# Front of a conditioned attention stack: partition maxima by TensorE, softmax bias by ScalarE, a symmetric score table made in part, new orders

## Chip, cores, metric

One core of a Trainium2 chip. The metric is the device time of one execution in microseconds. All eight batches are worked by this one core. Below, PE is TensorE, DVE VectorE, ACT ScalarE and POOL GpSimd.

## What is computed

The reference works on `x` of 8 x 256 x 256 (batch, tokens, features), in float32. Cut to what matters:

```python
# 1. conditioning: layer norms with gathered gains, six parts, MLP, layer norm
y = mlp_ln(concat([w0*h, w1*t, w2*m, w3*n, w4*r, w5*s]))
# 2. attention with L2-like similarity, 16 heads of 16
q_row_2 = max(sum(abs(q), -1), -1) ** 2          # per batch and head
k_col_2 = max(sum(abs(k), -2), -1) ** 2
denom = sqrt(sum(q*q)) * max(sum(abs(y), -2), -1)
sim = -(q_row_2 - 2*q@k.T + k_col_2) / denom
x1 = x + softmax(sim) @ v @ W_proj + b_proj
# 3. attention of each token over its own 16 heads; q = k = v = kx
kx = modulated_linear(x1, cond)                  # 16 heads of 16
scores[n, h, j] = sum_d kx[n, h, d] * kx[n, j, d] / 4
x2 = modulated_linear(softmax(scores) @ kx, cond)
# 4. six layers of windowed attention and gated MLP
return x1 + layers(x2)
```

`scores[n, h, j]` equals `scores[n, j, h]`. In `sim` the terms that depend on neither token are the same for a whole row.

## The kernel before

Three parts run one after the other, with a barrier of all engines between: `front` (steps 1 to 3), `local_layers` (step 4) and `write_out`.

In `front` each engine has a queue of its own, written by a loop over `t` in `range(FRONT_STEPS)`. Each stage has an offset: `pairs(t, off)` runs it in every step, for one pair of heads (64 pairs: 8 per batch), `batches(t, off)` in every eighth step, for one batch, `once` one time. Within a step the stages stand in the order of the lines of the loop. The queues are in-order and meet in semaphores only, so step 40 of one engine need not run beside step 40 of another. A batch passes through conditioning (a), attention (b) and the token's heads (c), and up to five batches are under way.

Stages that matter here, with their lines:

- Per pair of heads: PE `scores` (L559) makes 128x1024 scores; DVE `softmax` takes the maximum (`rmax`, L1107) and makes `rbias` of it in three operations of 128x4 (L1112 to L1114: times the scale, plus `offset`, minus `offset`); ACT `softmax` (L822) takes four exponentials of 128x256 with their sums; PE `flip_p` (L571) turns half of them into one bank, ACT `flip_p` (L831) copies that to `pr_t`, PE `weigh` (L584) multiplies by `v`. `scores` of pair j waits for the exponentials of pair j-2.
- Per batch, sizes of q, k and y: ACT sums into `qsq`, `kab`, `yab`; PE `sizes` (L541, L543) makes 16 matmuls of four columns and a sum over partitions; DVE puts 33 columns into `most` (128x33) and the norm into `fro` (L1085); POOL `scale_root` (L315) takes `fro` to the power -0.5, POOL `peaks` (L308) is a `partition_all_reduce` (maximum) of `most`; DVE `scales` (L1090 to L1097) makes `scl` and `offset`, 128x16 each.
- Conditioning: POOL `gather` (six indirect DMAs), `scale_h`, `scale_t`, `scale_s`, `affine_h` (elementwise, 128x512), PE `flip_x`, `flip_t`, `flip_s`, `flip_h` (L399), then `mixer_hidden` (L489, 32 matmuls of 256 columns). In the same queue of POOL stand `root` (L270), `dem_root` (L252, once), `turn_k` and `head_out` (L330).
- Heads of a token, per half u and quarter k: DVE `head_prod` (L1162, a product of 128x1024) and `head_scores` (L1169, its sum over 16, giving 128x64), then per half `head_peak`, ACT `head_exp`, DVE `head_weights`; then POOL `head_out` (L330) and DVE `head_out` (L1192) in turn.

PE's results of a whole batch share two banks, M0 and M1. `BANK0` and `BANK1` list their uses in order, and `after` makes a use wait for the copy of the one before it.

The write-out turns `state` by PE into one of two banks, ACT copies it into one of two row tiles, SP stores it.

## Time and profile before

| | |
|---|---|
| median of 3 runs | 3747.55 us (3742.12 to 3752.66) |
| profiled execution | 3748.91 us, span of its trace 3747.6 us |
| busy PE / DVE / ACT / POOL | 3447.7 / 2700.4 / 2549.3 / 2039.9 us |
| last `state` of the front begins | 827.7 us |
| first transpose of the write-out | 3734.2 us |
| granted clock of PE, mean | 0.934 |

The page cuts the span into 40 slices of 93.7 us; the digits of a slice are tenths of busy time, those of PEclk tenths of the full clock. PEld is PE's weight load, which overlaps PE. "Idle before" is what an engine stood still for ahead of an instruction, with the work that ended it; "issue" there means that nothing in the profile released it.

### The profile page before, as it was taken

Reading aid. Unit: us, or ns where it says so; the run is one execution under the profiler, and the core shown is the slowest. Engines: PE = TensorE matmul, PEld = TensorE weight load, DVE = VectorE, ACT = ScalarE, POOL = GpSimd, SP = SyncE. Lnnn points to the kernel's source line nnn. Section 1 sums busy time; section 2 is a strip of 40 time slices with the busy share of each in tenths; the row PEclk is TensorE's granted clock in tenths of the full one; section 3 lists DMA queues with packets and bytes.
Section 4 is the critical chain, followed back from the end, with each engine's and each line's share of the span. In section 5 each row is a group of like instructions: output and inputs, shape, how many; then the busy total and the mean of one; then the engine's idle time right before and its main releaser. Section 6 shows DMA issues by size and latency. Waiting matters only on the chain. (4 is left out here: it accounts for less than half of the span.)

```text
span 3747.6 us, 85444 instructions
## 1 busy us (share of the span) xinstructions
PE 3447.7 (92%) x32080; PEld 3019.9 (81%) x32080; DVE 2700.4 (72%) x5351; ACT 2549.3 (68%) x7091; POOL 2039.9 (54%) x1544
## 2 busy tenths in 40 slices
PE   5898889928999999999999999999999999999997
PEld 4787777716888888888888888888888888888886
DVE  2358777776777787777877778767787777877773
ACT  1554455406877777777777777777777777787774
POOL 5325453345655566555565555655556555565652
PEclk8687778658999999999999999999999999999998
DMA  3110000001000010000100001000010000100000
GB/s 112 50 32 29 29 29 4 4 20 49 18 2 2 10 45 19 2 2 10 40 24 2 2 10 37 27 2 2 10 37 27 2 2 10 37 26 7 4 7 23
DMA packets 26935, 75.60 MB, mean 20 GB/s; under 512 B 4025, under 2 KB 9753, under 8 KB 25497
## 3 DMA queue, kind: packets, MB, share of 16 engines
q1 hardware_dynamic: 21360, 52.89, 4.3%
q0 software_dynamic: 4864, 16.78, 1.4%
q8 instruction: 260, 4.26, 0.5%
q14 instruction: 147, 1.20, 0.1%
q10 hardware_dynamic: 304, 0.47, 0.0%
HBM read 65.94 MB, written 4.19 MB: 19 GB/s over the span
## 5 line engine op out<-in xcount | busy, mean ns | idle before, releaser
L1495 POOL TENSOR_TENSOR rnorm<-norm,half 128x8 f32<-128x8 f32 x384 | 684.4, 1782 | 1149.8 <-DVE norm L1927 1149.8
L1750 ACT ACTIVATE prob<-ps_s,ebias,rnorm 128x128 f32<-128x128 f32 x1536 | 681.3, 458 | 39.3 <-DVE ebias L1939 38.1
L1932 DVE TENSOR_REDUCE negmax<-ps_s 128x4 f32<-128x512 f32 x384 | 264.2, 688 | 404.8 <-PE ps_s L1574 404.4
L1497 POOL TENSOR_TENSOR turned<-by_cos,turned 128x512 f32<-128x512 f32 x384 | 515.3, 1342 | 0.0
L1740 ACT ACTIVATE qk_t<-ps_t 128x512 f32<-128x512 f32 x384 | 230.9, 601 | 271.4 <-PE ps_t L1545 271.4
L1520 PE MATMUL ps_qk<-w_hi,x_hi 128*128 128x512 f32 x768 | 333.1, 434 | 70.9 <-DVE turned L1919 56.8
L1614 PE MATMUL ps_f<-attn_t,w_o 128*128 128x128 f32 x3072 | 358.7, 275 | 0.0
L1614 PEld LDWEIGHTS ps_f<-attn_t,w_o 128*128 128x128 f32 x3072 | 350.5, 192 | 0.1
L1946 DVE TENSOR_TENSOR prob<-prob,rinv 128x512 f32<-128x512 f32 x384 | 322.2, 839 | 13.2
L1658 PE MATMUL ps_f<-lin_hi,w_hi 128*128 128x256 f32 (+1 forms) x1056 | 312.0, 295 | 6.4 <-DVE state L2008 6.4
L1750 ACT ACTIVATION_READ_ACCUMULATOR prob<-ps_s,ebias,rnorm 128x1 f32 x1536 | 315.3, 205 | 0.0
L1520 PE MATMUL ps_qk<-w_lo,x_hi 128*128 128x512 f32 x768 | 305.8, 398 | 0.0
L1723 ACT ACTIVATE sq<-ps_qk 128x512 f32<-128x512 f32 x384 | 230.0, 599 | 110.6 <-PE ps_qk L1520 107.3
L1520 PE MATMUL ps_qk<-w_hi,x_lo 128*128 128x512 f32 x768 | 304.3, 396 | 0.0
L1658 PE MATMUL ps_f<-lin_lo,w_hi 128*128 128x256 f32 (+1 forms) x1056 | 297.7, 282 | 0.0
L1500 POOL TENSOR_TENSOR turned<-turned,rnorm 128x256 f32<-128x256 f32 x384 | 280.3, 730 | 30.1
L1658 PE MATMUL ps_f<-lin_hi,w_lo 128*128 128x256 f32 (+1 forms) x1056 | 296.3, 281 | 0.0
L1919 DVE TENSOR_TENSOR turned<-ps_qk,sin_t 128x256 f32<-128x256 f32 x768 | 285.9, 414 | 0.0
L1759 ACT ACTIVATE prob_t<-ps_t 128x512 f32<-128x512 f32 x384 | 229.3, 597 | 60.1 <-PE ps_t L1583 60.1
L1913 DVE TENSOR_TENSOR by_cos<-ps_qk,cos_t 128x512 f32<-128x512 f32 x384 | 263.7, 687 | 3.7 <-ACT sq L1723 3.2
L1924 DVE TENSOR_REDUCE norm<-sq 128x8 f32<-128x512 f32 x384 | 259.5, 676 | 0.0
L1583 PE MATMUL ps_t<-ident,prob 128*128 128x128 f32 x1536 | 251.7, 286 | 4.4 <-DVE prob L1946 4.4
(263 smaller groups left out, 9685.4 us busy)
## 6 DMA issues: line engine op xcount, KB each, us to landing
w_raw<-in_w_qkv SPq DMA_DIRECT2D x24, 768.0 KB, 4.7
w_raw<-in_w SPq DMA_DIRECT2D x12, 693.0 KB, 4.5
w_o<-in_w_o SPq DMA_DIRECT2D x6, 1024.0 KB, 4.8
w_raw<-in_w SPq DMA_DIRECT2D x6, 768.0 KB, 4.2
x_tok<-in_x SPq DMA_DIRECT2D x8, 256.0 KB
kept<-x_t SPq DMA_DIRECT2D x8, 256.0 KB
w_raw<-kept SPq DMA_DIRECT2D x8, 256.0 KB, 2.7
out<-rows_out SPq DMA_DIRECT2D x8, 256.0 KB, 2.2
```

Of the source, the lines that this page charges most:

```text
L1495: G.tensor_tensor(rnorm[:, i % 4, :], norm2[:, k, :], half[:, :], ALU.pow).then_inc(s["rnorm"], 1)
L1497: G.tensor_tensor(turned[:, k, :], by_cos[:, k, :], turned[:, k, :], ALU.add).then_inc(s["turned"], 1)
L1500: G.tensor_tensor(kk, kk, rnorm[:, i % 4, GH:].unsqueeze(2).broadcast_to([P, GH, DH]), ALU.mult).then_inc(s["k_unit"], 1)
L1520: last = E.matmul(out, lhs.bitcast(F32R), w[:, kt, g, columns].bitcast(F32R), start=n == 0, stop=n == len(terms) - 1)
L1614: last = E.matmul(ps_f[0][:, mt * N + u * P:][:, 0:P], w_o[:, j, T(mt)], attn_t[:, j, T(u)], start=j == 0, stop=j == INNER // P - 1)
L1658: last = E.matmul(f[0:cut.stop - cut.start, part * N:(part + 1) * N], w[:, kt, cut].bitcast(F32R), x[:, kt, :].bitcast(F32R), start=n == 0 ...
L1750: last = A.activation(prob[:, k, h, :], half_bank(h % 2)[:, T(h // 2)], ACT.Exp, bias=ebias[:, k, h:h + 1], scale=rnorm[:, i % 4, h:h + 1] ...
L1913: V.tensor_tensor(by_cos[:, k, :].rearrange("p (a h d) -> p a h d", a=2, h=GH), qk[:, :].rearrange("p (a h d) -> p a h d", a=2, h=GH), cos ...
L1919: last = V.tensor_tensor(heads(turned[:, k, cut]), heads(qk[:, cut])[:, :, ::-1, :], sn.broadcast_to([P, GH, 2, DH // 2]), ALU.mult)
L1924: V.tensor_reduce(norm2[:, k, :], sq[:, k, :].rearrange("p (h d) -> p h d", d=DH), AX.X, ALU.add).then_inc(s["norm2"], 1)
L1932: V.tensor_reduce(negmax[:, k, :].rearrange("p (c o) -> p o c", o=2), ps_s[:, :, 0:2 * P].rearrange("p o (c k) -> p o c k", c=2), AX.X, AL ...
L1946: V.tensor_tensor(prob[:, k, :, :], prob[:, k, :, :], rinv[:, k, :].unsqueeze(2).broadcast_to([P, GH, P]), ALU.mult).then_inc(s["prob_unit ...
```

## The change

- Maxima over partitions: `peaks` goes. DVE still fills `most`; PE `flip_most` turns its columns into rows of 16 partitions (`M1`), with the sum of `qmask` behind them; DVE `take_peaks` takes the maxima there; POOL `scale_root` works on 16x1; DVE `scales` makes two columns of 16 partitions, and PE `scale_row` spreads them over 128 partitions; DVE `take_scales` copies them.
- Bias: DVE `softmax` keeps the maximum only. ACT makes `rbias` in two activations of 128x2 per pair, ahead of its exponentials, and waits for them on a semaphore.
- Heads: quarter k makes only the columns from 4k on (1024, 768, 512, 256 products). ACT `head_mirror` copies the other three blocks of each half (16, 32, 48 columns), and `head_peak` waits for it.
- Orders: all offsets and the order of the lines in the loops of POOL, PE, ACT, DVE are new, and so is the order of uses of M0 and M1; 142 steps.
- Write-out: eight banks and eight row tiles, and one semaphore.

```diff
...
-    m["most"], m["peak"] = sb("most", [P, 2 * NH + 1]), sb("peak", [P, 2 * NH + 1])
-    m["peak2"], m["yrec"] = sb("peak2", [P, 2 * NH]), sb("yrec", [P, 1])
-    m["offset"], m["qmask"] = sb("offset", [P, 2, NH]), sb("qmask", [P, NH])
-    m["fro"], m["scl0"], m["scl"] = sb("fro", [P, NH]), sb("scl0", [P, NH]), sb("scl", [P, 2, NH])
+    m["most"], m["peak"] = sb("most", [P, 2 * NH + 1]), sb("peak", [NH, 3])
+    m["peak2"], m["yrec"], m["scol"] = sb("peak2", [NH, 2]), sb("yrec", [NH, 1]), sb("scol", [NH, 2])
+    m["qmask"] = sb("qmask", [P, NH])
+    m["fro"], m["scl0"], m["scl"] = sb("fro", [NH, 1]), sb("scl0", [NH, 1]), sb("scl", [P, 2, 2 * NH])
...
-    m["prod"], m["prodo"] = sb("prod", [P, 2, 4, NH, HD]), sb("prodo", [P, 2, 4, HD, NH])
+    m["prod"], m["prodo"] = sb("prod", [P, 2, 4 * NH * HD]), sb("prodo", [P, 2, 4, HD, NH])
...
-FRONT_STEPS = 123
+FRONT_STEPS = 142
...
+    BANK0 = (("scale_row", 7, "scl", 1), ("mixer_hidden", 6, "hid", 1), ("flip_o", 8, "o_t", 1), ("dem_row", 8, "w_k", 1),
+             ("flip_y", 6, "y_t", 1), ("flip_heads", 10, "o2_t", 1), ("q1", 6, "q", 2), ("k1", 6, "k", 2), ("sizes", 6,
+             "most", 1), ("flip_x", 5, "x_t", 1), ("flip_s", 5, "cat_s", 1))
+    BANK1 = (("flip_h", 6, "cat_h", 1), ("mixer_out", 6, "y_b", 1), ("project_out", 8, "x1", 1), ("token_k", 8, "kx", 1),
+             ("q0", 6, "q", 2), ("heads_out", 10, "ostate", 1), ("k0", 6, "k", 2), ("project_v", 6, "v", 1), ("flip_t", 5,
+             "cat_t", 1), ("flip_most", 6, "peak", 1))
...
-        def peaks(a):
-            G.wait_ge(s["kmask"], a + 1)
-            G.wait_ge(s["fro"], a + 1)
+        def scale_root(a):
+            G.wait_ge(s["peak"], a + 1)
             if a:
-                G.wait_ge(s["scl"], a)
-            G.partition_all_reduce(m["peak"][:, :], m["most"][:, :], P, bass.bass_isa.ReduceOp.max
-                                   ).then_inc(s["peak"], 1)
-
-        def scale_root(a):
-            G.wait_ge(s["fro"], a + 1)
-            if a:
-                G.wait_ge(s["scl"], a)
-            G.tensor_tensor(m["scl0"][:, :], m["fro"][:, :], m["nhalf"][:, 0:NH], ALU.pow).then_inc(s["scl0"], 1)
+                G.wait_ge(s["scl_col"], a)
+            G.tensor_tensor(m["scl0"][:, :], m["fro"][:, :], m["nhalf"][0:NH, 0:1], ALU.pow).then_inc(s["scl0"], 1)
...
-            E.wait_ge(s["qmask"], a + 1)
             E.wait_ge(s["q_abs"], a + 1)
             after(BANK0, "sizes", a)
             for u in range(NU):
                 for t in range(NTILE):
-                    E.matmul(M0[:, NH * (1 + u) + 4 * t:][:, 0:4], m["q_abs"][:, t, T(u)], m["slots"][:, :],
-                             start=True, stop=True)
-            E.matmul(M0[:, 0:NH], m["ones"][:, :], m["qmask"][:, :], start=True, stop=True).then_inc(s["size_ps"], 1)
+                    last = E.matmul(M0[:, NH * u + 4 * t:][:, 0:4], m["q_abs"][:, t, T(u)], m["slots"][:, :],
+                                    start=True, stop=True)
+            last.then_inc(s["size_ps"], 1)
+
+        def flip_most(a):
+
+            most = m["most"]
+            E.wait_ge(s["qmask"], a + 1)
+            E.wait_ge(s["kmask"], a + 1)
+            E.wait_ge(s["most"], a + 1)
+            after(BANK1, "flip_most", a)
+            E.transpose(M1[0:NH, T(0)], most[:, 0:NH], ident[:, :])
+            E.transpose(M1[0:NH, T(1)], most[:, NH:2 * NH], ident[:, :])
+            E.matmul(M1[0:NH, T(2)], most[:, 2 * NH:].broadcast_to([P, NH]), ident[:, :], start=True, stop=True)
+            E.matmul(M1[0:NH, 3 * P:3 * P + 1], m["qmask"][:, :], m["ones"][:, 0:1], start=True, stop=True
+                     ).then_inc(s["most_ps"], 1)
+
+        def scale_row(a):
+            E.wait_ge(s["scl_col"], a + 1)
+            after(BANK0, "scale_row", a)
+            for k in range(2):
+                last = E.matmul(M0[:, k * NH:(k + 1) * NH], m["scol"][:, k:k + 1].broadcast_to([NH, P]), ident[0:NH, 0:NH],
+                                start=True, stop=True)
+            last.then_inc(s["scl_ps"], 1)
...
-            A.wait_ge(s["rbias"], j + 1)
+            A.wait_ge(s["rmax"], j + 1)
+            if hp == 0:
+                A.wait_ge(s["scl"], b + 1)
             if j >= 2:
+                A.wait_ge(s["exp"], j - 1)
                 A.wait_ge(s["prt_ps"], 2 * j - 2)
             if hp == 0 and b >= 2:
                 A.wait_ge(s["pri"], b - 1)
+            for e in range(2):
+                h = slice(2 * hp + e, 2 * hp + e + 1)
+                z = slice(NH + 2 * hp + e, NH + 2 * hp + e + 1)
+                last = A.activation(rbias[:, j % 2, e, :], rmax[:, j % 2, e, :], ACT.Identity, scale=scl[:, b % 2, h],
+                                    bias=scl[:, b % 2, z])
+            steps[0] += 1
+            last.then_inc(s["act_step"], 1)
+            A.wait_ge(s["act_step"], steps[0])
...
+        def head_mirror(c, u):
+            of = sc[:, 2 * (c % 2) + u, :, :]
+            A.wait_ge(s["hs"], 8 * c + 4 * u + 4)
+            for k in range(1, 4):
+                last = A.activation(of[:, 4 * k:4 * k + 4, 0:4 * k], of[:, 0:4 * k, 4 * k:4 * k + 4].rearrange("p j h -> p h j"),
+                                    ACT.Copy)
+            last.then_inc(s["hm"], 1)
...
         def take_sizes(a):
             V.wait_ge(s["size_ps"], a + 1)
             if a:
-                V.wait_ge(s["peak"], a)
+                V.wait_ge(s["most_ps"], a)
+            V.tensor_reduce(most[:, 0:NH], M0[:, 0:2 * NH].rearrange("p (u h) -> p h u", u=NU), AX.X, ALU.max
+                            ).then_inc(s["most"], 1)
+
+        def take_peaks(a):
+            V.wait_ge(s["most_ps"], a + 1)
+            if a:
                 V.wait_ge(s["scl0"], a)
-            V.tensor_reduce(most[:, 0:NH], M0[:, NH:3 * NH].rearrange("p (u h) -> p h u", u=NU), AX.X, ALU.max)
-            V.tensor_copy(m["fro"][:, :], M0[:, 0:NH]).then_inc(s["fro"], 1)
+                V.wait_ge(s["scl_col"], a)
+            V.tensor_reduce(m["peak"][:, :], M1[0:NH, 0:3 * P].rearrange("p (a n) -> p a n", a=3), AX.X, ALU.max)
+            V.tensor_copy(m["fro"][:, :], M1[0:NH, 3 * P:3 * P + 1]).then_inc(s["peak"], 1)
 
         def scales(a):
-            peak, peak2, sl, of = m["peak"], m["peak2"], scl[:, a % 2, :], offset[:, a % 2, :]
+
+            peak, peak2, col = m["peak"], m["peak2"], m["scol"]
             V.wait_ge(s["peak"], a + 1)
-            V.reciprocal(m["yrec"][:, :], peak[:, 2 * NH:])
-            done(V.tensor_tensor(peak2[:, :], peak[:, 0:2 * NH], peak[:, 0:2 * NH], ALU.mult))
+            if a:
+                V.wait_ge(s["scl_ps"], a)
+            V.reciprocal(m["yrec"][:, :], peak[:, 2:3])
+            done(V.tensor_tensor(peak2[:, :], peak[:, 0:2], peak[:, 0:2], ALU.mult))
+            done(V.tensor_tensor(col[:, 1:2], peak2[:, 0:1], peak2[:, 1:2], ALU.add))
+            V.wait_ge(s["scl0"], a + 1)
+            done(V.tensor_scalar(col[:, 0:1], m["scl0"][:, :], m["yrec"][:, 0:1], 2.0, ALU.mult, ALU.mult))
+            done(V.scalar_tensor_tensor(out=col[:, 1:2], in0=col[:, 1:2], scalar=0.5, in1=col[:, 0:1], op0=ALU.mult,
+                                        op1=ALU.mult))
+            V.tensor_tensor(col[:, 1:2], col[:, 1:2], col[:, 1:2], ALU.subtract).then_inc(s["scl_col"], 1)
+
+        def take_scales(a):
+            V.wait_ge(s["scl_ps"], a + 1)
             if a >= 2:
                 V.wait_ge(s["exp"], HP * (a - 1))
-            done(V.tensor_tensor(of, peak2[:, 0:NH], peak2[:, NH:], ALU.add))
-            V.wait_ge(s["scl0"], a + 1)
-            done(V.tensor_scalar(sl, m["scl0"][:, :], m["yrec"][:, 0:1], 2.0, ALU.mult, ALU.mult))
-            V.scalar_tensor_tensor(out=of, in0=of, scalar=0.5, in1=sl, op0=ALU.mult, op1=ALU.mult).then_inc(s["scl"], 1)
+            V.tensor_copy(scl[:, a % 2, :], M0[:, 0:2 * NH]).then_inc(s["scl"], 1)
 
         def softmax(j):
-            b, hp = divmod(j, HP)
-            k, of_heads = j % 2, [P, 2, NU]
-            sl = scl[:, b % 2, 2 * hp:2 * hp + 2].unsqueeze(2).broadcast_to(of_heads)
-            of = offset[:, b % 2, 2 * hp:2 * hp + 2].unsqueeze(2).broadcast_to(of_heads)
             V.wait_ge(s["sc_ps"], j + 1)
             if j >= 2:
                 V.wait_ge(s["exp"], j - 1)
-            V.tensor_reduce(rmax[:, k, :, :], SB[:, 2 * k:2 * k + 2, :].rearrange("p e (u n) -> p e u n", u=NU), AX.X, ALU.max,
-                            negate=True).then_inc(s["rmax"], 1)
-            V.wait_ge(s["rmax"], j + 1)
-            if hp == 0:
-                V.wait_ge(s["scl"], b + 1)
-            done(V.tensor_tensor(rbias[:, k, :, :], rmax[:, k, :, :], sl, ALU.mult))
-            done(V.tensor_tensor(rbias[:, k, :, :], rbias[:, k, :, :], of, ALU.add))
-            V.tensor_tensor(rbias[:, k, :, :], rbias[:, k, :, :], of, ALU.subtract).then_inc(s["rbias"], 1)
+            V.tensor_reduce(rmax[:, j % 2, :, :], SB[:, 2 * (j % 2):2 * (j % 2) + 2, :].rearrange("p e (u n) -> p e u n", u=NU),
+                            AX.X, ALU.max, negate=True).then_inc(s["rmax"], 1)
...
+        def among(k):
+
+            return prod[:, k % 2, :][:, 0:4 * (NH - 4 * k) * HD].rearrange("p (h j d) -> p h j d", h=4, d=HD)
+
         def head_prod(c, u, k):
             if u == 0 and k == 0:
                 V.wait_ge(s["kx"], c + 1)
             if c + u + k // 2:
                 V.wait_ge(s["hs"], 8 * c + 4 * u + k - 1)
-            kh, hs = kx[:, u, :].rearrange("p (h d) -> p h d", d=HD), slice(4 * k, 4 * k + 4)
-            V.tensor_tensor(prod[:, k % 2, :, :, :], kh[:, hs, :].unsqueeze(2).broadcast_to([P, 4, NH, HD]),
-                            kh.unsqueeze(1).broadcast_to([P, 4, NH, HD]), ALU.mult).then_inc(s["hp"], 1)
+            kh, shape = kx[:, u, :].rearrange("p (h d) -> p h d", d=HD), [P, 4, NH - 4 * k, HD]
+            V.tensor_tensor(among(k), kh[:, 4 * k:4 * k + 4, :].unsqueeze(2).broadcast_to(shape),
+                            kh[:, 4 * k:, :].unsqueeze(1).broadcast_to(shape), ALU.mult).then_inc(s["hp"], 1)
 
         def head_scores(c, u, k):
             V.wait_ge(s["hp"], 8 * c + 4 * u + k + 1)
             if c >= 2:
                 V.wait_ge(s["ho_prod"], 8 * (c - 2) + 4 * u + 4)
-            V.tensor_reduce(sc[:, 2 * (c % 2) + u, 4 * k:4 * k + 4, :], prod[:, k % 2, :, :, :], AX.X, ALU.add).then_inc(s["hs"], 1)
+            V.tensor_reduce(sc[:, 2 * (c % 2) + u, 4 * k:4 * k + 4, 4 * k:], among(k), AX.X, ALU.add).then_inc(s["hs"], 1)
 
         def head_peak(c, u):
-            V.wait_ge(s["hs"], 8 * c + 4 * u + 4)
+            V.wait_ge(s["hm"], 2 * c + u + 1)
...
-    rows_out = ctx.enter_context(nc.sbuf_tensor("rows_out", [P, 2, NU, D], F32))
-    bank = [ctx.enter_context(nc.psum_tensor(f"out_bank{k}", [P, 512], F32)) for k in range(2)]
-    s = Signals(nc, ctx, "end", "flipped rows stored0 stored1")
+    rows_out = ctx.enter_context(nc.sbuf_tensor("rows_out", [P, B, NU, D], F32))
+    bank = [ctx.enter_context(nc.psum_tensor(f"out_bank{k}", [P, 512], F32)) for k in range(B)]
+    s = Signals(nc, ctx, "end", "flipped rows stored")
...
```

New order of POOL in the steps of one period (steps 80 to 87; in brackets the batch, for head_out then half and quarter): 80 head_out(0; 1,0), head_out(0; 1,1), scale_t(4), affine_h(4); 81 gather(5); 82 head_out(0; 1,2); 84 scale_root(3), head_out(0; 1,3); 85 turn_k(1); 86 head_out(1; 0,0), (0,1), root(4,y), root(5,x), scale_h(5), head_out(1; 0,2), scale_s(5); 87 head_out(1; 0,3), root(5,h).

PE around the boundary: 86 project_v(4); 87 weigh, sizes(4), flip_t(5), flip_p, flip_x(5), weigh, scores, flip_most(4), flip_p, flip_s(5); 88 weigh, flip_h(5), flip_p, weigh, scores, scale_row(4), flip_p, mixer_hidden(5). DVE: 85 head_out(1; 0,3); 86 h_norm(5), take_sizes(4); 87 head_out(1; 1,0), yk_most(4), softmax, take_peaks(4), scales(4); 88 take_scales(4). At the start POOL has dem_root ahead of root(0,x) in step 46, and scale_root(0) in step 60, behind affine_h(1) in 56 and gather(2) in 57.

## Rows read from the trace of the kernel before

**Rows 1.** The page, 40 slices of 93.7 us: busy tenths and granted clock.

```profile
PE   5898889928999999999999999999999999999997
PEclk8687778658999999999999999999999999999998
```

**Rows 2.** Windows: length, busy us of PE, PEld, DVE, ACT, POOL, clock, DMA.

```profile
98.70:166.60 67.90, 58.30 (x324) 49.17 (x323) 23.46 (x65) 38.51 (x115) 21.80 (x20) 0.75 0.10 32
166.60:241.00 74.40, 73.78 (x418) 64.63 (x417) 37.02 (x79) 43.45 (x123) 24.69 (x21) 0.78 0.11 37
...
324.80:415.10 90.30, 76.24 (x399) 65.92 (x398) 64.37 (x106) 44.05 (x126) 44.56 (x29) 0.74 0.08 27
...
673.20:731.00 57.80, 50.84 (x260) 42.98 (x260) 47.30 (x71) 27.05 (x77) 21.06 (x10) 0.65 0.01 5
731.00:829.00 98.00, 33.60 (x116) 26.57 (x116) 82.21 (x80) 12.95 (x29) 52.11 (x22) 0.56 0.01 3
```

**Rows 3.** Timeline of POOL at one batch boundary: start us, us, instruction, idle before.

```profile
405.25 3.83 POOL L315 TENSOR_TENSOR scl<-fro,nhalf 128x16 f32<-128x16 f32 x1 [9.86 <-DVE fro L1085]
415.13 0.47 POOL L308 PARTITION_ALL_REDUCE peak<-most  x1 [6.05 <-issue]
422.62 2.31 POOL L330 TENSOR_TENSOR prodo<-sc,kd 128x1024 f32<-128x1024 f32 x1 [7.02 <-issue]
424.90 1.25 POOL L284 TENSOR_TENSOR hh<-hh,ct 128x512 f32<-128x512 f32 x1
```

**Rows 4.** Timeline of PE at the same boundary.

```profile
417.24 0.66 PE L571 MATMUL bank_pb<-ident,pr 128*128 128x128 f32 x4
427.56 1.12 PE L399 MATMUL bank_m<-ident,hh 128*128 128x128 f32 x4 [9.66 <-POOL hh L285]
```

**Rows 5.** Waits of the front (0 to 860 us): us in total, times, longest.

```profile
ACT pr_t L831 <- PE bank_pb L571: 151.9, 72, 10.0
...
PE bank_m L399 <- POOL hh L285: 55.8, 7, 11.3
...
POOL peak L308 <- issue: 47.1, 8, 6.0
```

**Rows 6.** Windows of 10 us around the same boundary.

```profile
400.00:410.00 10.00, 10.00 (x49) 9.46 (x48) 5.36 (x11) 6.98 (x28) 3.83 (x1) 0.56 0.01 2
...
430.00:440.00 10.00, 10.00 (x48) 9.14 (x48) 9.93 (x9) 5.48 (x14) 4.42 (x2) 0.50 0.00 1
```

**Rows 7.** Timeline of POOL at the start of the front.

```profile
74.63 5.42 POOL L252 TENSOR_TENSOR dem<-dem_v,nhalf 128x32 f32<-128x32 f32 x1
```

**Rows 8.** Groups by line and form, 0 to 860 us: count | busy, mean ns | idle.

```profile
L1162 DVE TENSOR_TENSOR prod<-kx 128x1024 f32<-128x1024 f32 x64 | 88.4, 1387 | 0.0
...
L1169 DVE TENSOR_REDUCE sc<-prod 128x64 f32<-128x1024 f32 x64 | 77.4, 1210 | 0.0
...
L1113 DVE TENSOR_TENSOR rbias<-rbias,offset 128x4 f32<-128x4 f32 x64 | 27.1, 423 | 2.2
...
L768 ACT ACTIVATE y_t<-bank_m,fcols 128x256 f32<-128x256 f32 x16 | 8.2, 560 | 14.8 <-PE bank_m L399 14.8
...
L714 ACT ACTIVATE m_hid<-bank_ob,fcols 128x8 f32<-128x8 f32 x6 | 1.1, 274 | 18.2 <-PE bank_ob L406 18.2
```

**Rows 9.** Timeline of DVE, one bias operation by itself.

```profile
457.62 0.16 DVE L1113 TENSOR_TENSOR rbias<-rbias,offset 128x4 f32<-128x4 f32 x1
```

**Rows 10.** Groups of DVE by form in the drain, 731 to 829 us.

```profile
L1162 DVE TENSOR_TENSOR prod<-kx 128x1024 f32<-128x1024 f32 x13 | 22.7, 1756 | 0.0
L1169 DVE TENSOR_REDUCE sc<-prod 128x64 f32<-128x1024 f32 x14 | 16.9, 1206 | 0.0
```

**Rows 11.** Timeline of the write-out.

```profile
3734.20 3.74 PE L2091 MATMUL out_bank<-ident,state 128*128 128x128 f32 x16 [1.96 <-PEq L2076]
...
3738.23 0.60 ACT L2100 ACTIVATE rows_out<-out_bank 128x512 f32<-128x512 f32 x1 [1.45 <-DMA out<-rows_out]
...
3738.88 1.97 PE L2091 MATMUL out_bank<-ident,state 128*128 128x128 f32 x8 [0.94 <-ACT rows_out L2100]
```

551 lines of the change are left out of this document (275 added, 276 removed).

## Prediction

> **What bounds the kernel now.** I read the page first, by its 40 slices [rows 1]. From about 910 us on (slice 10) TensorE (PE) is at 9 tenths and its granted clock at 9 or more: that is the six layers, and no edit touches them. The first nine slices, up to 829 us, are the front, where PE's digit is 8 or 9 but the clock moves between 5 and 8. So the front is where time can come from; the write-out behind the layers is the only other place.
>
> Second view: the front cut at the eight starts of the partition all-reduce, one per batch [rows 2]. The seven periods sum to 574.5 us (98.7 to 673.2), then 57.8 us until the last maximum of the scores and 98 us of drain. In a full period (324.8 to 415.1) PE is busy 76.2 of 90.3 us at a clock of 0.74, VectorE (DVE) 64.4, ScalarE (ACT) 44.0, GpSimd (POOL) 44.6. None is full: it is a pipeline of in-order queues that stops somewhere. In the drain DVE is busy 82.2 of 98 us and PE 33.6: there DVE is the bound.
>
> Third view, where it stops: POOL's timeline [rows 3] and PE's [rows 4] at one batch boundary. POOL waits 9.9 us for `fro`, takes 3.8 us for a power over 128x16, stands 6.05 us before the all-reduce with nothing released (issue), 0.47 us in it, and then 7.02 us more before its next instruction: 17.4 us from 405.25 to 422.62 for one batch's peaks. `affine_h` of the next batch is queued behind that; PE's `flip_h` waits for it 9.66 us. The waits of the whole front [rows 5] say that it is so in every batch: 47.1 us of issue before the eight all-reduces, 55.8 us of PE behind `hh`.
>
> Fourth view: what the stall costs beyond itself. Four `flip_p` transposes take 0.66 us before it and the four of `flip_h` 1.12 us after it [rows 4]: the granted clock has gone from 2.4 to 1.2 GHz. It is still 0.50 from 430 to 440 us, with PE busy throughout [rows 6]. An earlier fall belongs to `sizes` (from 401 us, 16 matmuls of four columns): mean 0.56 from 400 to 410 us. In a period of length T with mean clock c, T(1-c) is the time lost to the low level: 90.3 x 0.26 = 23.5 us from 324.8 on, 74.4 x 0.22 = 16.4 us from 166.6 on [rows 2]. Taking this and PE's idle time (14.1 and 0.6 us) away leaves 53 and 57 us of PE work at the full clock; part of the idle time lies in the low level and is taken off twice, so I take 58.
>
> **The change part by part.**
>
> *Peaks.* Removed from POOL: the all-reduce with its 6 us before and 7 us behind, and the power over 16 columns (3.8 us [rows 3]). In its place: one power over 16x1. A power over 128x32 takes 5.4 us and over 128x16 3.8 [rows 3, 7], so 0.1 us per column and about 2.2 fixed by these two, which is the upper end; zero is the lower. The all-reduce's own 0.47 shows that POOL has cheaper instructions. I take 0.7, below the middle, since the path now feeds 16 lanes in place of 128. PE gets three turns, one column of sums, two row spreads, and loses the two `ones` matmuls of `sizes`: four more at about 0.3 us (the four 128-column transposes of `flip_h` take 1.12 us at the low clock [rows 4]), with waits +1.5 us per batch. DVE gets `take_peaks`, one more small operation in `scales`, and `take_scales`: five at about 0.16 us [rows 9], under 1 us. The chain from `sizes` to `scl` is then: take_sizes, flip_most, take_peaks, root, four small DVE steps, scale_row, take_scales, about 4 us if every engine is free, against 10.4 us on POOL alone now (405.25 to 415.60).
>
> Are they free? POOL's new order puts before `scale_root` of batch a: head_out(1,0), head_out(1,1), scale_t and affine_h of a+1, gather of a+2 (six issues and a copy, some 8.5 us), head_out(1,2). A `head_out` product takes 2.31 us, an elementwise operation of 512 columns 1.25 [rows 3]. Counted from DVE's step 85, where the last release of these falls, that is 4.6 + 2.5 + 2.5 + 8.5 + 2.3 = 20.4 us, against two steps and a half (of 9 us each, an eighth of a period: 22 us) until `take_peaks`. So `scales` waits between 0 and 6 us; DVE and, one step later, ACT's softmax wait with it, and PE's `scale_row` stands in front of flip_p and the mixer. I take 3 us of PE idle per batch in place of some 13.
>
> *Bias by ACT.* DVE loses three 128x4 operations per pair. One takes 0.16 us when alone [rows 9], but the middle one 0.42 us on average, 27.1 us in all [rows 8]: between 0.5 and 1.3 us per pair, and I take 1.0, with the gaps 8.3 us per batch. ACT gets two activations of 128x2 with both scale and bias from memory. The rows [rows 8] give 0.27 us for 128x8 with a bias, and 0.56 us for 128x256 with both, so 0.27 to 0.56 and, since two columns are nearer to eight than to 256, 0.33; two with the wait on themselves 0.7 us, 5.6 us per batch, 45 us in all. ACT goes from 44 to 50 us per period, then 52 with the mirror: covered as long as the period is above 60. The Trainium skill speaks against this edit: "ScalarE: Activation LUTs", section "Rules for kernel authors", gives adds and multiplies to VectorE, since ScalarE's fixed cost per instruction is the higher. By the rows it is, 0.3 against 0.16 us; the fixed figures of that page of the Trainium skill would give about 0.37 us each, an estimate from its 186 ns and 93 ns for each of the two operands, with which ACT would still be covered and the sum the same. That rule is rival 3 here: what matters is who waits in ACT's queue.
>
> *40 of 64 columns.* The 64 products (1.387 us) and 64 sums (1.210 us) of 1024 elements [rows 8] become 1024, 768, 512 and 256. With 0.15 us fixed (by the 0.16 us of a tiny operation [rows 9]) the mean of an undisturbed 1.21 us falls to 0.81: 128 x 0.40 = 51 us less DVE in all, 6.4 per batch. ACT gets three copies per half (16 to 48 columns, 0.3 us each), 1 us, and `head_peak` waits for them, once per half, about 1.3 us in the chain of a batch's heads. Steady state: DVE 64 - 8.3 - 6.4 = 50 us per period, so it was no bound and is none; the gain of both DVE edits is worth nothing there except for shorter waits in between. Their cover gone, in the drain, they count in full.
>
> *New orders.* `project_v` comes before `sizes`; all between `sizes` and the mixer stays thin (flips of 128 and weights of 16 columns). So I keep one fall of the clock per batch there: of the 16 to 24 us lost per period, 11 stay. At the start `dem_root` (5.4 us at 74.6 us [rows 7]) is now ahead of root x of batch 0, where it was behind everything, and the first `scale_root` is behind the second gather: together the first softmax comes 5 us later.
>
> *Write-out.* Eight banks and eight row tiles in place of two. Now: 13.4 us from the first transpose to the end, since from the third batch on each pair waits for a store, ACT 1.45 us each time [rows 11]. After: 32 transposes at the measured 1.97 us per 8 are 7.9 us, then 0.6 of ACT and 2.2 of the last store (the page's time to landing of the stores to `out`): 10.7. Bounds: 9 us if stores and ACT hide all but PE, 13.4 if eight stores together are slower than one. I take -3.
>
> **The sum.** Start +5. Periods: PE work 58, new matmuls 1.5, idle 3, clock 11 make 74 for the five full periods; 66 and 70 for the two first (67.9 and 74.4 now, no heads yet). 506 in place of 574.5: -68. Last batch -8 (its low clock is 0.65, and DVE, busy 47.3 of 57.8 us, is relieved of 14 us). Drain: 13 products and 14 sums lie in it [rows 10]: 27 x 0.375 x 1.07 = 11 us, half of the 0.55 us by which the products (1.756 us) are held up there (3.5), the last bias 1.7, and 2 for shorter chains: -18. Write-out -3. Together -92. The profiled execution took 3748.91 us (span 3747.6, 1.4 above the median of the runs): 3748.9 - 92 = 3657.
>
> **The rivals.**
>
> 1. *A wait takes the stall's place.* If POOL comes to `scale_root` some 10 us late each batch, PE idles at `scale_row`, and the clock falls twice per batch as now: period about 83 for the full ones, -10 to -15 in the seven. With the other terms: -39, 3710 us. For it: the order above, and POOL's 9.9 us of waiting in front of its root now [rows 3]. Against: with 41 us of work POOL has some 30 us of idle time per period once the all-reduce is gone.
> 2. *The clock holds.* With no stall PE stays at 2.4 GHz through `sizes` too: period 63, -133 in the seven, -157 in all, 3592 us. For it: most of the low level now lies behind the stall. Against: in the second period PE is busy 73.8 of 74.4 us, without a stall, and the clock is still 0.78 [rows 2].
> 3. *ACT becomes the queue that stops, and the kernel slower.* The mirror waits for the sums (DVE) in ACT's in-order queue; behind it are `flip_p` copies, and PE's one bank of turned probabilities waits for these. ACT's copies already wait 151.9 us for PE [rows 5], so they have slack. The second mirror of a batch stands in ACT's step 72, its last sums in DVE's step 73 behind `y_add`, which waits for PE. There are 16 mirrors: from 92/16 = 5.8 us of blocked PE at each on, all is lost; at 10 us each the time is 3657 + 160 = 3817 us. Against: PE takes up the next probabilities a step later, and the first mirror has its sums a step ahead.
> 4. *Nothing moves:* the order, not POOL, holds the period. Then only the write-out and half of the drain (POOL's eight products of 2.3 us bound its end) count against the start: +5 - 9 - 3 = -7, 3742 us.
>
> **How the numbers follow.** Forecast (3630 to 3685) 0.55, rival 1 0.22, rival 2 0.14, rival 3 0.04, rival 4 0.05. The unknown costs (root 0 to 2.2 per batch, ACT 0.54 to 1.12 per pair, write-out -4 to 0) move the sum by some 10 us; period and clock by 4 us per period, 28. The range runs from 3600 (most of rival 2 below it is left out) to 3708 (half of rival 1 inside). A measurement of this kernel tells about 0.3%, 11 us: faster 0.92, within 0.04 (most of rival 4), slower 0.04.
>
> **What would show it.** Right: POOL free of the 17 us hold; `flip_h` on PE waiting under 2 us; starts of `scale_row` 72 to 77 us apart in full periods; DVE near 50 us per period; front's end (last `state` of the front) near 740 us; the last 13.4 us now under 11. Wrong: waits of PE on `scol` or of DVE on `scl0` over 5 us per batch (rival 1), mean clock over 0.9 in the periods (rival 2), ACT waiting for DVE's `sc` above 5 us with PE idle on `pr_t` (rival 3).

## The result, and the profile after

| | before | after |
|---|---|---|
| median | 3746.31 us (3742.12 to 3752.66) | 3602.68 us (3601.89 to 3603.45) |
| ratio of the two | | 0.9615, 95% interval 0.9599 to 0.9632 |
| span of the profiled execution | 3747.6 us | 3602.1 us |
| granted clock of PE, mean | 0.934 | 0.959 |

The change takes 144 us, 3.85%. Forecast were 92 us and 3657 us; the range (3600 to 3708) holds the time by 2.7 us. By the spans, 143 of the 145.5 us lie in the front and the write-out. The page of the kernel after, its slices of 90 us (to compare with [rows 1]): the clock now reaches 9 tenths in two slices of the front.

```profile
PE   4999999389999999999999999999999999999997
PEclk8789987699999999999999999999999999999998
```

Windows of the kernel after, cut at the eight `scale_root` and then at the last maximum of the scores and the last `state`, with the columns of [rows 2]:

```profile
103.10:167.48 64.38, 59.94 (x326) 51.57 (x327) 18.11 (x42) 44.77 (x131) 18.89 (x19) 0.77 0.15 49
167.48:235.61 68.13, 67.49 (x406) 58.54 (x405) 31.10 (x62) 46.74 (x136) 19.82 (x20) 0.83 0.14 40
235.61:303.62 68.01, 67.77 (x424) 59.69 (x423) 48.35 (x85) 49.19 (x147) 38.12 (x28) 0.85 0.11 38
303.62:368.85 65.23, 63.87 (x436) 56.05 (x434) 50.58 (x85) 51.11 (x153) 40.46 (x30) 0.94 0.13 42
368.85:432.94 64.09, 62.35 (x412) 55.18 (x414) 52.95 (x84) 49.82 (x148) 40.42 (x29) 0.92 0.12 42
...
561.76:608.78 47.02, 44.21 (x261) 38.48 (x260) 34.71 (x53) 31.66 (x97) 19.76 (x9) 0.72 0.02 6
608.78:688.22 79.44, 35.51 (x126) 28.58 (x126) 57.28 (x70) 14.92 (x42) 47.27 (x20) 0.56 0.01 4
```

A full period is 63 to 65 us in place of 90, and PE is busy in nearly all of it: PE is now the bound. The seven periods end at 561.76, so they take 458.7 us in place of 574.5. The terms of the span, before against after: start +4.4 (98.70, the first all-reduce, to 103.10, the first root; the first exponential goes from 101.9 to 107.7 us), periods -115.8, last batch -10.8, drain -17.3 (731.00 to 827.7 against 608.78 to 688.22), layers -2.3, write-out -3.8: together the 145.5 us between the spans, to the rounding.

POOL's timeline at one batch boundary, for [rows 3]: `affine_h` of the next batch, (six DMA issues,) a product of a head, the root over 16x1, the next product. The 17.4 us hold is gone.

```profile
356.77 1.26 POOL L284 TENSOR_TENSOR hh<-hh,ct 128x512 f32<-128x512 f32 x1
...
366.57 2.33 POOL L321 TENSOR_TENSOR prodo<-sc,kd 128x1024 f32<-128x1024 f32 x1
368.85 0.57 POOL L306 TENSOR_TENSOR scl<-fro,nhalf 16x1 f32<-16x1 f32 x1
```

Waits of the front (0 to 720 us), for [rows 5]. PE's wait for `hh` is not in the list any more, ACT's for PE has gone from 151.9 to 32.0 us, and the two that my rivals 1 and 3 named are small: DVE for POOL's root 2 us per batch, the mirror (`sc` L867) for DVE twice.

```profile
ACT pr_t L855 <- PE bank_pb L580: 32.0, 33, 2.2
...
DVE scol L1140 <- POOL scl L306: 14.3, 7, 5.1
...
ACT sc L867 <- DVE sc L1215: 11.4, 2, 9.3
...
PE bank_m L550 <- DVE scol L1143: 6.6, 3, 3.2
```

Groups of the front by form, for [rows 8]: ACT's bias and DVE's longest product.

```profile
L838 ACT ACTIVATE rbias<-rmax,scl 128x2 f32<-128x2 f32 x128 | 42.4, 384 | 30.9 <-DVE scl L1149 21.2 <-issue 9.7
L1208 DVE TENSOR_TENSOR prod<-kx 128x1024 f32<-128x1024 f32 x16 | 23.9, 1492 | 0.3
```

The write-out, for [rows 11]: 32 transposes without a stop, 9.65 us from here to the span's end at 3602.1 in place of 13.4.

```profile
3592.45 6.12 PE L2139 MATMUL out_bank<-ident,state 128*128 128x128 f32 x32 [1.96 <-PEq L2126]
```

### The profile page after: what moved, and what is told of

The parts are those of the page before. It is cut to its first block and busy times, and to the rows that moved or that the text cites. A ratio compares the mean times of both kernels' runs of the same rounds, so it can differ in the third digit from the quotient of the medians.

```text
span 3602.1 us, 85564 instructions
## 1 busy us (share of the span) xinstructions
PE 3383.3 (94%) x32144; PEld 2970.1 (82%) x32144; DVE 2583.0 (72%) x5183; ACT 2595.5 (72%) x7267; POOL 2014.8 (56%) x1536
## 5 line engine op out<-in xcount | busy, mean ns | idle before, releaser
L321 POOL TENSOR_TENSOR prodo<-sc,kd 128x1024 f32<-128x1024 f32 x64 | 162.4, 2548 | 180.3 <-DVE o L1238 98.5
```

## The experiments

All times are medians; each ratio is to the kernel before, run on the same chip. Us saved is (1 - ratio) x 3748. Differences between the runs are given by this column unless the text says that they are of medians.

| | orders | maxima | DVE's work | us | ratio, interval | saved |
|---|---|---|---|---|---|---|
| before | old | all-reduce | old | 3746 | | |
| before_copied_peaks | old | none, a copy | old | 3676.3 | 0.9799 (0.9773, 0.9825) | 75 |
| before_turned_peaks | old | turned | old | 3750.3 | 1.0009 (0.9997, 1.0021) | -3 |
| before_light_dve | old | all-reduce | light | 3713.2 | 0.9902 (0.9871, 0.9934) | 37 |
| old_work_new_orders | new | all-reduce | old | 3670.0 | 0.9791 (0.9768, 0.9813) | 78 |
| after_dve_work_back | new | turned | old | 3654.9 | 0.9745 (0.9716, 0.9773) | 96 |
| after_old_peaks | new | all-reduce | light | 3613.7 | 0.9638 (0.9622, 0.9654) | 136 |
| after_all_columns | new | turned | bias by ACT | 3628.8 | 0.9668 (0.9633, 0.9703) | 124 |
| after_bias_by_dve | new | turned | 40 columns | 3629.6 | 0.9669 (0.9636, 0.9703) | 124 |
| after | new | turned | light | 3602.7 | 0.9615 (0.9599, 0.9632) | 144 |
| after_filler | new | turned | light | 3584.1 | 0.9553 (0.9534, 0.9572) | 168 |
| after_root_first | new, 2 moves | turned | light | 3577.8 | 0.9540 (0.9520, 0.9559) | 172 |
| after_row_sizes | new | turned, other `sizes` | light | 3577.7 | 0.9535 (0.9518, 0.9552) | 174 |
| rows_and_root_first | new, 2 moves | turned, other `sizes` | light | 3574.0 | 0.9534 (0.9517, 0.9551) | 175 |

The new write-out (3.8 us by the trace, not run by itself) goes with the new orders.

### Which part is it?

**Maxima alone, in the old orders.** First the all-reduce taken out (what it computes is left out), then the turned maxima put in, at places that I chose in the old orders.

```diff
-            G.partition_all_reduce(m["peak"][:, :], m["most"][:, :], P, bass.bass_isa.ReduceOp.max
-                                   ).then_inc(s["peak"], 1)
+            G.tensor_copy(m["peak"][:, :], m["most"][:, :]).then_inc(s["peak"], 1)
```

> The kernel before with one instruction changed: POOL copies most into peak (128x33) in place of the all-reduce over partitions, so each partition keeps its own maximum (this part of the computation is left out). The power over 128x16 and all orders stay. Theory A (POOL's stand around the all-reduce, and the low clock behind it, is most of the gain): about 13 us of the 17.4 us hold go in each of eight batches, of which 8 to 13 us reach the period; 3746 becomes 3645 to 3680 us. Theory B (the new orders are most of the gain): 3725 us or more. Theory C (less work for DVE is most of it): 3725 us or more as well.

> The kernel before with the turned maxima alone: flip_most, take_peaks, scale_root on 16x1, scale_row and take_scales put into the old orders; bias by DVE, 64 columns and the old write-out stay. Theory A: 3640 to 3670 us, the period 72 to 77 us. Theory B: 3720 us or more. Theory C: 3720 us or more. If it stays above the run with the copied maxima by over 15 us, the longer way through PE and DVE costs what POOL gives back.

Theory A held for the first and fell with the second. Windows between two roots, the kernel with the copy first, the one with turned maxima second; below them PE's wait in the second, from 230 to 560 us (us, times, longest), then what DVE and POOL did ahead of one of these waits:

```profile
367.77:446.30 78.53, 71.22 (x410) 61.85 (x409) 69.07 (x107) 44.47 (x127) 45.60 (x30) 0.83 0.12 34
```
```profile
411.21:499.84 88.63, 78.81 (x418) 67.64 (x416) 71.84 (x110) 44.59 (x126) 41.03 (x28) 0.73 0.10 31
```
```profile
PE bank_m L551 <- DVE scol L1121: 22.4, 4, 7.0
```
```profile
411.43 3.85 DVE L1116 TENSOR_TENSOR scol<-peak 16x1 f32<-16x1 f32 x1
...
415.56 1.06 DVE L1119 SCALAR_TENSOR_TENSOR scol<-scol 16x1 f32<-16x1 f32 x1
416.65 2.25 DVE L1121 TENSOR_TENSOR scol<-scol 16x1 f32<-16x1 f32 x1
```
```profile
411.21 0.55 POOL L307 TENSOR_TENSOR scl<-fro,nhalf 16x1 f32<-16x1 f32 x1 [13.01 <-DVE fro L1106]
411.73 2.32 POOL L322 TENSOR_TENSOR prodo<-sc,kd 128x1024 f32<-128x1024 f32 x1
414.02 1.25 POOL L284 TENSOR_TENSOR hh<-hh,ct 128x512 f32<-128x512 f32 x1
415.35 1.26 POOL L285 TENSOR_TENSOR hh<-hh,ct 128x512 f32<-128x512 f32 x1
416.57 2.32 POOL L322 TENSOR_TENSOR prodo<-sc,kd 128x1024 f32<-128x1024 f32 x1
```

Without the all-reduce the period goes from 90.3 to 78.5 us: the hold did bound the kernel before. With the turned maxima in its place it is 88.6: PE's wait for `hh` is replaced by one for `scol`, up to 7.0 us, with the clock at 0.73.

This looks like my rival 1, but it is not: POOL was not late. It had stood for 13.01 us when `fro` came, and took the root at once. What was slow is DVE's chain behind it. Three operations over 16x1 took 3.85, 1.06 and 2.25 us; the same three take 0.15 us each in the kernel after (median of the eight batches). Each of the three ends within 0.02 us of an operation of POOL: at 415.28, 416.62 and 418.90 us, where POOL's `hh`, `hh` and product end at 415.27, 416.61 and 418.89. The excess is 6.7 us, and PE's wait there is 6.57. It is the same in the periods that begin at 322.8 and 499.8 us. So the place that I chose put DVE's chain beside POOL's products and `hh`, which the new orders do not: there POOL's next product after the root begins only at 373.79 us, when the chain is done. That another place in the old orders would have let the turned maxima pay was not tried.

**The new orders with all the old work**, and **the changed kernel with the old maxima.** (In the second the offset stays in the bias; it is the same for a whole row.) The code of the old work stands at the places of the new:

```diff
             for q in batches(t, 60):
                 scale_root(q)
+                peaks(q)
...
-            for q in batches(t, 55):
-                flip_most(q)
-            for q in batches(t, 56):
-                scale_row(q)
```

> The changed kernel with all of the old work put back in the new orders: all-reduce and power over 128x16 by POOL in the place of the new scale_root, bias by DVE, 64 columns, no mirror; only orders and write-out are new. Theory A: 3700 to 3750 us, since POOL still holds 17 us per batch. Theory B: 3610 to 3650 us. Theory C: 3690 to 3730 us.

> The changed kernel with the old maxima alone put back (sizes with its sum by ones, power over 128x16 and all-reduce by POOL, scales on 128x16); bias by ACT, 40 columns and the new orders stay. Theory A: 75 to 110 us come back, 3678 to 3713 us, and the clock in the periods falls to about 0.80. Theory B: under 20 us come back, up to 3623 us. Theory C: the same as theory B.

Both fell outside what theory A gave; the first (3670 us) fell outside the ranges of all three theories, the second (3613.7) into that of B and C. With all of the old work the orders alone save 78 us; and with everything but the maxima 136 of the 144 are there. The hold is nearly as long as it was. POOL's timeline in the new orders with the old work:

```profile
448.06 1.26 POOL L284 TENSOR_TENSOR hh<-hh,ct 128x512 f32<-128x512 f32 x1
...
459.94 2.95 POOL L314 TENSOR_TENSOR scl<-fro,nhalf 128x16 f32<-128x16 f32 x1
468.76 0.47 POOL L307 PARTITION_ALL_REDUCE peak<-most  x1 [5.88 <-issue]
476.37 2.31 POOL L329 TENSOR_TENSOR prodo<-sc,kd 128x1024 f32<-128x1024 f32 x1 [7.13 <-DVE o L1205]
```

16.4 us from the root to the next product, against 17.4 in [rows 3]. But `affine_h` (L284) of the next batch now stands ahead of it, done at 449.3, where in the old orders it was queued behind it. So PE's `flip_h` has its data, and the hold is felt by DVE, which waits for `peak`, and a few stages later by PE's `flip_o`. DVE's row, and PE's two longest waits from 230 to 560 us; the third block is PE's longest wait in the same stretch of the kernel before:

```profile
469.34 0.16 DVE L1096 RECIPROCAL yrec<-peak 128x1 f32<-128x1 f32 x1 [13.01 <-POOL peak L307]
```
```profile
PE bank_m L397 <- DVE o L1134: 29.7, 5, 8.9
PE bank_m L397 <- DVE v_rows L1064: 9.0, 4, 2.3
```
```profile
PE bank_m L399 <- POOL hh L285: 38.9, 4, 11.3
```

None of it is for `hh`, which was the main one in the old orders. Which of the many moves counts was not tried one by one; the rows show that the wait for `hh` went and the waits for `o` and `v_rows` came, and these two are together as long (38.7 us). DVE's late `o` is work of DVE, so a lighter DVE should pay here.

The 78 us of the orders are near the 75 us of the copy, but they are not the same ones. All of PE's waits from 230 to 560 us sum to 50.6 us before, to 29.6 with the copy and to 45.6 with the new orders. The last five of the seven periods (between roots) take 432 us before, 379 with the copy and 387 with the new orders. The new orders get 21 us behind the last root, where the copy gets 5. So moving `affine_h` ahead of the hold is not shown to do what removing the hold does.

**DVE's edits**, in the old orders, and taken back in the new ones, together and one by one.

```diff
+            done(V.tensor_tensor(rbias[:, k, :, :], rmax[:, k, :, :], sl, ALU.mult))
+            done(V.tensor_tensor(rbias[:, k, :, :], rbias[:, k, :, :], of, ALU.add))
+            V.tensor_tensor(rbias[:, k, :, :], rbias[:, k, :, :], of, ALU.subtract).then_inc(s["rmax"], 1)
...
-                            kh[:, 4 * k:, :].unsqueeze(1).broadcast_to(shape), ALU.mult).then_inc(s["hp"], 1)
+                            kh.unsqueeze(1).broadcast_to(shape), ALU.mult).then_inc(s["hp"], 1)
```

> The kernel before with DVE's two edits alone, in the old orders: bias by ACT, 40 columns, a mirror by ACT at the old place of the sums; maxima by the all-reduce, old write-out. Theory D (DVE's work lies on the path that turns one batch into the next, so taking it away pays in any order): as with the new orders, 50 to 60 us less, 3685 to 3700 us. Theory E (the old orders hold the period, DVE's work counts only once they are gone): only the drain's 10 to 20 us, 3725 to 3740 us.

> The changed kernel with all of DVE's old work put back: bias by three operations of DVE, 64 columns, no mirror; turned maxima and new orders stay. Theory D with maxima that are worth some 10 us in any company: 3655 to 3665 us. Rival (with DVE's work back, the all-reduce's place is on the path, and the turned maxima are worth much more than they are beside a light DVE): 3610 to 3640 us. Theory A as I forecast it (POOL's stand is most of the gain, and DVE's edits count in the drain only) gives 3615 to 3625 us.

> The changed kernel with 64 columns in place of 40 and no mirror by ACT. DVE gets 6.4 us per batch back. My forecast's reading (hidden in the periods, in the drain it counts): 8 to 15 us more, 3611 to 3618 us. Theory D (DVE's work is on the path in the periods as well): 25 to 45 us more, 3628 to 3648 us.

> The changed kernel with the softmax bias made by DVE in three operations of 128x4 (eight columns of 45 us of ACT's work go, 8 us per batch of DVE's come back). My forecast's reading: within 5 us, 3598 to 3608 us. Theory D: 15 to 30 us more, 3618 to 3633 us, since the bias stands between the scores and the exponentials of every pair, and PE waits for these two pairs later.

In the new orders the two are worth 48 us beside the turned maxima (96 against 144) and 57 beside the all-reduce (78 against 136); one by one 20 each, by the ratios. Theory D holds there. In the old orders they are worth 37 us, between theory D's 50 to 60 and theory E's 10 to 20; 28 of them lie in the seven periods (573.3 to 545.6 us between the first and the last root). The period of after_dve_work_back, and PE's longest wait from 230 to 560 us in it:

```profile
390.06:464.88 74.82, 69.94 (x417) 60.88 (x416) 65.27 (x108) 44.55 (x126) 42.00 (x29) 0.82 0.11 36
```
```profile
PE bank_m L388 <- DVE v_rows L1079: 15.7, 4, 4.9
```

DVE's work rises by 12.3 us per period (52.95 to 65.27) and the period by 10.7 us, though DVE is idle for 9.5 us of it. PE idles 4.9 us in place of 1.7, and the clock goes from 0.92 to 0.82: T(1-c) from 5.1 to 13.5 us. Most of the loss is the clock's.

**And the maxima?** after_old_peaks against after is 136 against 144 us, with intervals that overlap; in the trace the periods of the kernel with the old maxima sum to 461.3 us and those of the one after to 458.7. But they are not the same ones. Windows of the second and the fifth period, old maxima in the new kernel:

```profile
160.63:220.16 59.53, 58.89 (x404) 52.52 (x404) 31.05 (x58) 47.36 (x138) 22.77 (x21) 0.96 0.15 45
...
360.31:431.91 71.60, 67.94 (x410) 59.83 (x409) 50.95 (x82) 50.34 (x148) 43.58 (x30) 0.83 0.12 37
```

The full period is 7.5 us longer than after the change, the second one 8.6 us shorter, with the clock at 0.96 where it is 0.83 after the change. So the turned maxima paid in the full periods, and something took it back in the early ones.

### The clock

In the kernel after PE is busy throughout the second period (67.49 of 68.13 us), so its 0.83 is no matter of waits. Windows of 4 us after `sizes` (157.95 to 159.9), first of the kernel after, then of the one with filler:

```profile
163.48:167.48 4.00, 4.00 (x19) 2.57 (x20) 1.79 (x4) 2.11 (x8) 0.00 (x0) 0.50 0.19 66
...
175.48:179.48 4.00, 4.00 (x12) 3.37 (x13) 2.60 (x8) 3.45 (x11) 0.00 (x0) 0.50 0.00 0
```
```profile
161.00:165.00 4.00, 4.00 (x35) 3.34 (x34) 0.65 (x4) 3.03 (x8) 0.00 (x0) 1.00 0.65 195
...
173.00:177.00 4.00, 4.00 (x20) 3.51 (x19) 0.00 (x0) 0.78 (x3) 0.00 (x0) 1.00 0.00 0
```

Busy 4.00 of 4.00 in both, at 1.2 GHz in the one and at 2.4 GHz in the other. Three kernels were made to ask why. (The matmul in the loop of `sizes` runs eight times, and the trace shows it as 16 instructions; the four of the other form below are eight in the trace, and so are the filler's four.)

```diff
+                    if u:
+                        E.matmul(M0[:, N:2 * N], m["q_abs"][:, t, T(u)], m["q_abs"][:, t, :], start=True, stop=True)
                     last = E.matmul(M0[:, NH * u + 4 * t:][:, 0:4], m["q_abs"][:, t, T(u)], m["slots"][:, :],
```

> The changed kernel with eight matmuls of 128x256 added to sizes, one beside each of the last eight thin ones, into columns of the bank that nobody reads (work added, no result changed). At the full clock one takes 0.236 us, so 1.9 us per batch, 15 us in all. Theory F (the low clock of 3 to 20 us per batch after sizes comes of the thin matmuls there): the clock of the periods rises, and the time is 3585 to 3605 us. Rival (the low clock has another cause): 3612 to 3622 us, with the clock of each period as after the change.

```diff
-                    last = E.matmul(M0[:, NH * u + 4 * t:][:, 0:4], m["q_abs"][:, t, T(u)], m["slots"][:, :],
-                                    start=True, stop=True)
+                last = E.matmul(M0[0:NH, 0:N], m["slots_of"][:, t, :], m["q_abs"][:, t, :], start=t == 0, stop=t == NTILE - 1)
```

> The changed kernel with sizes turned round: four matmuls with 16 columns of weights and 256 of q_abs, summed in PSUM, in place of 16 with four columns; the result has the heads on 16 partitions at once, so the first of flip_most's three turns goes and take_sizes is one maximum of 16x256. PE's work falls from 1.93 us to about 0.95 us per batch, 8 us in all, and flip_most by 0.2 us. Theory F: the clock falls for less time behind sizes too, 15 to 35 us less than after the change, 3568 to 3588 us. Rival (only the work counts): 6 to 10 us less, 3593 to 3597 us.

```diff
+            for q in batches(t, 57):
+                scale_root(q)
             for q in batches(t, 41):
                 gather(q)
-            for q in batches(t, 60):
-                scale_root(q)
```

> The changed kernel with two moves in POOL's order alone: scale_root ahead of the gather of the next batch (offset 57 in place of 60), dem_root behind root h of batch 0 in place of ahead of root x. If the start term of my forecast (+5 us for the late first softmax) and the waits of DVE for POOL's root (14.3 us in seven batches after the change) stand on the path: 8 to 16 us less than after the change, 3587 to 3595 us. Rival (PE is busy all along in the periods, so these waits are covered): within 4 us, 3598 to 3606 us. Against both: POOL waits for the peaks ahead of the gather, and the next batch's tables come late: over 3610 us.

> Both edits together: sizes as four matmuls with 16 columns of weights, scale_root ahead of the gather and dem_root behind root h of batch 0. If the two gains (25 us each) are of different things they add up: 3548 to 3558 us. If both buy back the same stretches at the low clock (in both the second period fell from 68 to 57 or 58 us, which I think the likelier): the shorter of the two in each period gives some 14 us less than either, 3558 to 3570 us. If nothing is left to gain: 3574 to 3580 us.

With 64 matmuls more the kernel is 23 us faster (19 by the medians; 0.9553 against 0.9615, intervals apart), 1 us below what theory F gave. With `sizes` in the other form it is 30 us faster (25 by the medians), as theory F had it, and here PE's work did not fall as I had expected: the eight wide instructions take 1.90 us where the 16 thin ones took 1.93, and only a turn of `flip_most`, 0.2 us, goes. So less work is not the reason. `sizes` after the change and in the other form:

```profile
157.95 1.93 PE L529 MATMUL bank_m<-slots,q_abs 128*128 128x4 f32 x16
```
```profile
158.94 1.90 PE L529 MATMUL bank_m<-q_abs,slots_of 128*16 128x256 f32 x8
```

The second and fourth period, first with filler, then with `sizes` in the other form, then with the root ahead of the gather:

```profile
166.51:226.09 59.58, 59.58 (x414) 52.55 (x414) 32.23 (x62) 46.19 (x137) 19.93 (x19) 0.97 0.14 45
...
289.58:354.36 64.78, 62.67 (x428) 54.93 (x426) 53.36 (x87) 49.60 (x148) 40.42 (x30) 0.97 0.13 41
```
```profile
165.91:224.34 58.43, 57.79 (x397) 49.85 (x396) 31.33 (x62) 46.19 (x138) 19.67 (x19) 0.97 0.14 44
...
289.49:354.78 65.29, 62.15 (x407) 53.21 (x407) 50.60 (x85) 49.61 (x148) 40.40 (x29) 0.95 0.13 41
```
```profile
163.01:219.94 56.93, 56.30 (x406) 49.66 (x405) 31.72 (x62) 46.15 (x137) 19.73 (x19) 1.00 0.15 47
...
278.88:342.81 63.93, 63.93 (x426) 56.65 (x425) 51.89 (x86) 49.90 (x149) 40.56 (x29) 0.92 0.13 42
```

after_root_first gives 25 us by the medians, more than the 8 to 16 that I expected if POOL's waits were on the path. Its first root comes 1.5 us earlier (101.64 in place of 103.10), a full period is about as long as after the change; 20.3 of the 25 us are the second and third period (68.13 and 68.01 to 56.93 and 58.94), where the clock rose to 1.00 and 0.94.

This run bears on theory F too. PE's instructions and their order are those of the kernel after, thin `sizes` included (155.99 to 157.9 us), and the clock stays up behind them:

```profile
157.00:161.00 4.00, 4.00 (x37) 3.67 (x36) 0.54 (x4) 3.41 (x11) 0.00 (x0) 1.00 0.08 17
```

Over the eight batches, the clock falls within 8 us of the start of `sizes`, with PE busy for over 7.7 of the 8 us, six times after the change, three times in after_root_first, and never with filler, with `sizes` in the other form, or with both edits. So theory F holds as far as this: the clock fell right behind `sizes` only where its thin matmuls stand there with no wide one among them, but they do not always bring the fall. In the second period `sizes` begins 2 us earlier and the gather comes behind it; what of this keeps the clock up is not shown.

The three edits do not buy back quite the same stretches. The second period is 9 to 11 us shorter in each; beyond it the root's move gets 9.1 us in the third period and 2.5 in the seventh, the other `sizes` 2.9 and 8.4. Both together (rows_and_root_first) give 3574.0 us, 4 less than either by the medians and within the intervals: they do not add up, and the gain of 14 us that I thought the likelier did not come either. The pair keeps the 10.2 us of the third period and only 3.2 of the seventh; why is not shown. It is the fastest version here, 0.8% under the changed kernel. Its full periods are 62 to 65 us, no shorter; PE is busy for 60 to 63 us of each.

The transfers are no cause: in after_filler the gather falls into the same microseconds as after the change (195 GB/s from 161 to 165 us), and the clock is 1.00; and after the change the clock falls behind the `sizes` of the seventh batch too, when nothing is moved:

```profile
488.00:492.00 4.00, 4.00 (x22) 3.96 (x20) 1.38 (x4) 2.74 (x6) 2.34 (x1) 0.50 0.00 0
```

## Why the prediction came out as it did

- **What bounds the kernel before:** right for that kernel. The hold around the all-reduce set its period; without it 75 us go (before_copied_peaks), 12 us per full period.
- **The step that failed** is the attribution in *Peaks*: "I take 3 us of PE idle per batch in place of some 13" was booked as the work of the turned maxima. In the new orders they bring 8 us beside the light DVE and 18 beside the old, neither well resolved, since 78 us are there by the orders with the hold in place. In the old orders they bring nothing (before_turned_peaks): the chain was taken as "four small DVE steps", free if every engine is free, and three of them took 7.2 us beside POOL's operations. I had listed the new order of POOL, with `affine_h` four steps ahead of the root, and used it only to ask whether the root would be late. *New orders* put a price on the start (+5) and on the clock (11 us), and none on the waits that the moves themselves take away.
- **DVE's edits:** "worth nothing there except for shorter waits in between" is wrong. In full periods 12.3 us less work made them 10.7 us shorter, by less idle time of PE (1.7 us for 4.9) and by a higher clock (0.92 for 0.82). The durations were near: DVE's sum fell as forecast (64 to 50.6 us; forecast 50), ACT's bias took 0.384 us (forecast 0.33), the mirror copies 0.23 to 0.28. The Trainium skill, "ScalarE: Activation LUTs", gives about 0.37 us for the bias as an estimate from its fixed figures, and the trace agrees with 0.384; its "Rules for kernel authors" would keep this multiply and add on VectorE (for the speed per element; the higher fixed cost that the prediction gives as the reason is in the rows, 0.27 against 0.16 us), and there the run decides the other way: with the bias on DVE the kernel is 20 us slower, and ACT had the room (busy 49.8 of 64.1 us in a full period).
- **The clock term was too large.** Of 74 us per full period, 58 and 1.5 were work of PE: measured 65.23 us less 1.36 idle and 3.9 of T(1-c) is 60.0. Idle was put at 3 and the low clock at 11; they are 1.4 and 3.9 there, 1.7 and 5.1 in the next. That is nearly all of the 9 us by which the full periods are shorter than 74. In the sum this is the miss: the five full periods were put at 370 us and took 326, 44 of the 52 us between forecast and result. The two early periods (66 and 70 forecast, 64.4 and 68.1 measured) came out near, but held 10 to 14 us that each of the small edits takes away.
- **The small terms** were right: start +4.4 for +5, last batch -10.8 for -8, drain -17.3 for -18, write-out -3.8 for -3, root over 16x1 0.57 us for 0.7.
- **The signs:** DVE's 50 us and the last 13.4 us under 11 came as said. The periods (63 to 65 us for 72 to 77) and the front's end (688 us for 740) did not, and the clock above 0.9, named as the sign of rival 2, came in three periods.
- **The rivals:** rival 1 (POOL late for its root) did not happen: DVE waits 2 us per batch for the root in the new orders, and in the old ones, where PE idled at `scale_row`, POOL was on time. Its price was off too: 83 us for a full period makes -17 us in the five, not -10 to -15. Rival 2 (3592 us) was nearest to the time: the clock held above 0.9 in three of the full periods, not in the early ones. Rival 3 did not come: PE waited 5.6 us in all for `pr_t`. Rival 4 (the order, not POOL, holds the period) had the right lever and the wrong sign; it was read as "nothing moves", though the orders were part of the change.

So the time fell into the range by luck, 2.7 us from its edge, with the causes shared out wrongly: too much to the maxima, nothing to the orders and to DVE in the periods.

## What to carry to other kernels

When an engine holds its queue for long, look also at what stands behind it: here new orders with the hold in place saved as much (78 us) as removing it in the old orders (75), and in them the turned maxima brought only 8 to 18 us more. Where a chain of tiny operations goes through DVE, look at what POOL does at the same time: operations of 0.15 us took up to 3.85. Where PE waits for other engines, work taken from DVE can shorten the period nearly one for one (12.3 us less work, 10.7 us; DVE was busy for 87% of that period). And where PE is busy but at 1.2 GHz, try its thin matmuls in fewer and wider ones: in this kernel that gave 25 us by the medians for 16 of them per batch, though they took PE as long as before (1.90 us for 1.93).
